# Five orders changed in a two-layer transformer kernel: queries and keys ahead of values in the first stage's middle chunks, and four reorderings further on

## The reference

```python
x = _layernorm(x + _L0_attn_ref(x, ...))  # 16 heads; half of each query and key gets rotary positions; causal softmax
x = _layernorm(x + _L0_ffn_ref(x, ...))   # shared expert plus the 2 best of 8 experts by sigmoid(x @ gate_w.T) + bias
x = _layernorm(x + _L1_attn_ref(x, ...))  # one head of width 512, biases, rotary positions on all of q and k
x = _layernorm(x + _L1_ffn_ref(x, ...))   # h = silu(x @ w_gate) * (x @ w_up); keep 2 of each 4 by size; h @ w_down
...
q_sem, k_sem = _split_heads(x @ Wq_sem.T, H), _split_heads(x @ Wk_sem.T, H)
q_geo, k_geo = _rope(_split_heads(x @ Wq_geo.T, H)), _rope(_split_heads(x @ Wk_geo.T, H))
v = _split_heads(x @ Wv.T, H)
```

## Time and profile before

| | |
|---|---|
| three runs | 2268.37, 2268.38 and 2271.72 us, median 2268.38 us |
| the profiled execution | span 2270.2 us; its own time 2271.96 us |
| PE busy in the span | 2172.7 us, 96% |
| DVE, ACT, POOL busy | 1191.6, 753.1, 670.4 us |
| mean granted clock of PE | 0.983 of full |
| layer0_qkv | 0 to 148.4 us |
| layer0_attention and layer0_project | 148.4 to 837 us |
| layer0_experts | 837 to 1149 us |
| layer1_attention | 1149 to 1713 us |
| layer1_mlp | 1713 to 2270 us |

### The profile page before, as it was taken

How to read it: one execution, slowest core, us unless ns; L and a number is a source line. 1 busy time by engine, 2 the same in 40 slices (tenths; PEclk the granted TensorE clock), 3 DMA queues, 4 the chain that set the end, 5 groups by cost and what they waited for, 6 DMA issues and landing times. The chain is left out here.

```text
span 2270.2 us, 27500 instructions
## 1 busy us (share of the span) xinstructions
PE 2172.7 (96%) x10148; PEld 1497.2 (66%) x10148; DVE 1191.6 (52%) x2324; ACT 753.1 (33%) x1351; POOL 670.4 (30%) x458
## 2 busy tenths in 40 slices
PE   8999999999999899999979999999998999999997
PEld 6876555555553644444457778888877888888885
DVE  6877677676661643222247542322236546554666
ACT  3325555555556332111134321111223221211223
POOL 5345555555556105332223250000003021211200
PEclk9989999999999999999999999999999999999999
DMA  5478245343300625555534460000101010100001
GB/s 198 176 204 199 81 118 132 95 89 71 71 15 21 247 79 211 136 115 90 85 105 142 149 231 20 28 19 19 47 1 56 1 38 19 38 18 18 19 19 56
DMA packets 104605, 197.27 MB, mean 87 GB/s; under 512 B 10385, under 2 KB 27665, under 8 KB 103057
## 3 DMA queue, kind: packets, MB, share of 16 engines
q1 hardware_dynamic: 92064, 162.78, 24.5%
q0 software_dynamic: 11408, 29.69, 5.8%
q10 hardware_dynamic: 1008, 3.15, 0.4%
HBM read 123.82 MB, written 71.75 MB: 86 GB/s over the span
## 5 line engine op out<-in xcount | busy, mean ns | idle before, releaser
L684 ACT ACTIVATE a_probs<-a_stb 128x512 f32<-128x512 f32 (+3 forms) x640 | 309.8, 535 | 240.6 <-PE a_stb L825 126.4
L650 POOL TENSOR_TENSOR a_probs<-a_probs 128x1024 f32<-128x1024 f32 (+3 forms) x158 | 278.4, 1775 | 247.5 <-PE a_avb L837 233.6
L722 DVE TENSOR_REDUCE a_mparts<-a_sbank 128x1 f32<-128x512 f32 x384 | 240.0, 683 | 86.3 <-PE a_sbank L799 86.1
L2207 POOL CAST m_wh<-wst 128x1024 fp32r<-128x1024 f32 x24 | 26.7, 1112 | 720.8 <-POOLq L1510 368.9
L57 PE MATMUL m_gu<-hi,m_wh 128*128 128x512 f32 x512 | 200.5, 392 | 4.7 <-DVE m_h L2282 2.8
L58 PE MATMUL m_gu<-lo,m_wh 128*128 128x512 f32 x512 | 199.9, 390 | 0.0
L59 PE MATMUL m_gu<-hi,m_wl 128*128 128x512 f32 x512 | 199.8, 390 | 0.0
L837 PE MATMUL a_avb<-a_probs,V 128*32 128x512 f32 (+3 forms) x1280 | 151.6, 546 | 0.7 <-ACT a_probs L684 0.7
L2282 DVE TENSOR_TENSOR m_h<-m_sg,m_gu 128x512 f32<-128x512 f32 x64 | 44.0, 688 | 193.8 <-ACT m_sg L2237 193.5
L727 DVE CUSTOM_DVE_ANT_0 a_junk<-a_sbank,hidden 128x128 bf16<-128x128 f32 (+3 forms) x256 | 113.4, 488 | 55.9 <-PE a_sbank L799 54.4
L799 PE MATMUL a_sbank<-hi,q 96*128 96x512 f32 (+3 forms) x304 | 119.4, 418 | 7.6 <-DVE a_mparts L722 4.2
(11 more groups left out here) (284 smaller groups left out, 4761.3 us busy)
## 6 DMA issues: line engine op xcount, KB each, us to landing
qk<-v_hl SPq DMA_DIRECT2D x32, 512.0 KB, 3.0
hi<-qk SPq DMA_DIRECT2D x60, 256.0 KB, 5.1
lo<-qk SPq DMA_DIRECT2D x60, 256.0 KB, 5.3
wst<-in_w_mlp SPq DMA_DIRECT2D x24, 512.0 KB, 3.5
q<-qk SPq DMA_DIRECT2D x42, 256.0 KB, 5.8
xs<-a_zeros POOLq DMA_DIRECT2D x39, 264.0 KB, 2.8
X<-xs SPq DMA_DIRECT2D x39, 264.0 KB, 2.7
v<-vhl SPq DMA_DIRECT2D x16, 512.0 KB, 5.1
```

Source lines behind the costliest of these rows:

```text
L650: nc.gpsimd.tensor_tensor(probs[:, i % PSLOTS, hs, w0:], probs[:, i % PSLOTS, hs, w0:], probs[:, (i + 1) % PSLOTS, hs, w0:], ALU.add)\
L684: nc.scalar.activation(probs[:, i % PSLOTS, h, w0:], stb[:, k % 3, w0:], ACT.Exp, scale=SCALE0)\
L722: nc.vector.reduce_max(to, sbank[:, b, :], AX).then_inc(s["unit_max"], 1)
```

## The change

Nothing is computed otherwise; five orders are changed.

1. layer0_qkv. In chunks 1 and 2 all four q/k groups are multiplied first (with the input event ahead of the last), then the four value tiles; so too in chunk 3, where the first value tile stood behind the second group. Chunk 0 keeps its order. ACT makes "high" one event later, DVE makes "low" behind the next group's shuffle. Piece 3 of the weights goes from POOL to ACT and DVE, and POOL splits pieces 2 and 4, then, behind the first cosines, 5.
2. layer0_project. "ranks" stands behind the event ("w", 3, 0) and not ahead of ("b", 1, 0).
3. The last two indirect additions, not one, are issued in layer1_attention.
4. layer1_attention. Other orders of ACT and DVE in its front and its chunks; bvr is loaded first.
5. layer1_mlp. In the first quarter DVE's product m_h of (c, r) = (1, 0) stands behind the first of the four low parts m_hl, not behind the fourth.

```diff
 layer0_qkv
+                if c > 0:
+                    return [("qk", c, 0), ("qk", c, 1), ("qk", c, 2), ("x", c + 1, 0), ("qk", c, 3)] + [("v", c, t) for t in range(TC)]
                 return ev + [("x", c + 1, 0), ("v", c, 1), ("qk", c, 3), ("v", c, 2), ("v", c, 3)]
-            return ev + [("qk", c, 3), ("v", c, 1), ("v", c, 2), ("v", c, 3)]
+            return [("qk", c, j) for j in range(NG)] + [("v", c, t) for t in range(TC)]
...
             split(2)
-            split(3)
+            split(4)
             for what, c, j in events:
                 if what == "qk":
                     cosines(c, j)
-                    if c == 0 and j < 2:
-                        split(4 + j)
+                    if c == 0 and j == 0:
+                        split(5)
...
-            last_qk = events.index(("qk", NC - 1, NG - 1))
-            acts = events[:last_qk + 3] + [("high", NC - 1, NG - 1)] + events[last_qk + 3:]
+            acts = []
+            for i, ev in enumerate(events):
+                acts.append(ev)
+                if i > 0 and events[i - 1][0] == "qk":
+                    acts.append(("high", *events[i - 1][1:]))
...
+                            if i == 4:
+                                split(3)
...
+            for i, (what, c, j) in enumerate(events):
+                swapped = [ev for ev in events[:i] if ev[0] == "qk"][-1:] if what != "v" else []
+                held = [("low", *ev[1:]) for ev in swapped if ("low", *ev[1:]) not in steps]
+                if what == "qk":
+                    steps += [("swap", c, j)] + held + [("sum", c, j)]
+                elif what == "x":
+                    steps += [("x", c, j)] + held
+            steps.append(("low", NC - 1, NG - 1))
 layer0_project
-            ev += [("ranks", 0, -1)] * before + [("b", 1, 0), ("w", 3, 0)]
+            ev += [("b", 1, 0), ("w", 3, 0)] + [("ranks", 0, -1)] * before
 layer0_experts and layer1_attention (LATE = 2)
-            for j in range(NR - 1):
+            for j in range(NR - LATE):
...
-            pool.wait_ge(added, 16 * (NR - 1))
-            nc.gpsimd.indirect_dma_start(acc_dram[:, :], bass.IndirectOffsetOnAxis(ap=last_to, axis=0), last_rows, None,
-                                         compute_op=ALU.add).then_inc(added, 16)
+            for i in range(LATE):
+                pool.wait_ge(added, 16 * (NR - LATE + i))
+                nc.gpsimd.indirect_dma_start(acc_dram[:, :], bass.IndirectOffsetOnAxis(ap=last_to[i], axis=0), last_rows[i],
+                                             None, compute_op=ALU.add).then_inc(added, 16)
 layer1_attention, DVE in a chunk (ACT likewise)
-                if c + 1 < NC:
-                    stats(n)
-                    stats(n + 1)
-                    apply(n)
-                    apply(n + 1)
-                sines(p)
...
+                for t, tiles in enumerate(((n,), (n + 1, n + 2), (n + 3,))):
+                    sines(p + t)
+                    for k in tiles if c + 1 < NC else ():
+                        stats(k)
+                    sums(p + t)
+                    for k in tiles if c + 1 < NC else ():
+                        apply(k)
+                    low(p + t)
 layer1_mlp
+                            if c == 0 and r == 0 and is_first(q):
+                                dve.wait_ge(s["hl_ok"], 1)
+                                dve.wait_ge(s["sg_ok"], 5)
+                                tt(h[:, 0, :], sg[:], gu[:, 0, 1, :], ALU.mult).then_inc(s["h_ok"], 1)
```

More of the change, by code:

```diff
@@ L293, in split @@
             def split(i):
-                act.wait_ge(wload[i], 16)
-                nc.scalar.activation(piece_of(i, wqh, wvh), wst[:, i, :], ACT.Copy).then_inc(s["whi_a"], 1)
+                act.wait_ge(wload[i % 3], 16 * (i // 3 + 1))
+                nc.scalar.activation(piece_of(i, wqh, wvh), wst[:, i % 3, :], ACT.Copy).then_inc(s["whi_a"], 1)
             def split_half(a):
@@ L330, in _ @@
                     nc.scalar.activation(qkf[:, k % 2], qk[:, k % 2], ACT.Copy).then_inc(s["qkf_ok"], 1)
-                if what == "high" or (what == "qk" and k < NC * NG - 1):
+                elif what == "high":
                     act.wait_ge(s["sum_ok"], k + 1)
@@ L358, in _ @@
             split_half(0)
-            for what, c, j in events:
+            steps = []
+            for i, (what, c, j) in enumerate(events):
[6 more added lines that the diff above has]
+            steps.append(("low", NC - 1, NG - 1))
+            for what, c, j in steps:
                 k = c * NG + j
@@ L368, in _ @@
                         split(1)
-                elif what == "qk":
+                        split(3)
+                elif what == "swap":
                     dve.wait_ge(s["qkf_ok"], k + 1)
@@ L373, in _ @@
                     nc.vector.stream_shuffle(rotated[:], qkf[:, k % 2], SWAP).then_inc(s["rot_ok"], 1)
+                elif what == "sum":
                     if j == 0:
@@ L381, in _ @@
                     tt(t1[:, k % 2], t1[:, k % 2], rotated[:], ALU.add).then_inc(s["sum_ok"], 1)
+                elif what == "low":
                     dve.wait_ge(s["hi_ok"], k + 1)
@@ L914 @@
 AHEAD = 2
+LATE = 2
 def shared_up(nc, w0, xt, ab, c, j):
@@ L1033, in run @@
                         act.wait_ge(s["gt_ok"], g + 1)
+                        if not opening:
+                            act.wait_ge(s["sm_ok"], g)
                         nc.scalar.activation(sig[:].rearrange("p t e -> p (t e)"), sb8[:, 0:TC * NE],
@@ L1496, in _ @@
             down(NR - 1, old)
-    return s["added"], y[:, (NR - 1) % 2, :], to[:, NR - 1:NR]
+    late = range(NR - LATE, NR)
+    return s["added"], [y[:, j % 2, :] for j in late], [to[:, j:j + 1] for j in late]
 READY = 12
@@ L1721, in _ @@
                 weight(0, d)
+            fuse(0)
             act.wait_ge(s["bias_in"], 16)
             nc.scalar.activation(bvh, bvr[:].unsqueeze(2).broadcast_to([P, ND, P]), ACT.Copy).then_inc(s["bvh_ok"], 1)
-            fuse(0)
-            weight(1, 0)
-            weight(1, 1)
             fuse(1)
-            weight(1, 2)
-            weight(1, 3)
+            fuse(2)
+            for d in range(ND):
+                weight(1, d)
+            fuse(3)
+            nc.scalar.activation(nrm.std[:, NT - 1:NT], nrm.eps[:], ACT.Sqrt)
+            fuse(ND)
             root(0)
-            fuse(2)
             apply(0)
             root(1)
+            apply(1)
             turn(0)
-            apply(1)
-            fuse(3)
             root(2)
+            apply(2)
             turn(1)
-            apply(2)
-            fuse(ND)
             root(3)
@@ L2028, in scores @@
                     last.then_inc(s["s_ok"], 1)
-            for j in range(3):
+            for j in range(ND + 1):
                 fuse(j)
             turn(0)
-            fuse(3)
             turn(1)
-            fuse(ND)
             value(0)
@@ L2278, in run @@
                     elif what == "up":
+                        if (c, r) == (1, 0) and is_first(q):
+                            continue
                         if r == 0 and not (c == 0 and is_first(q)):
+                            dve.wait_ge(s["hl_ok"], i * 4)
+                        if r == 1 and c == 1 and is_first(q):
                             dve.wait_ge(s["hl_ok"], i * 4)
```

55 lines of the change are left out of this document (21 added, 34 removed).

## The result

The changed kernel takes 2278.35 us in the median of 6 runs (2277.6 to 2286.03), the kernel before 2270.05 in the median of 6 (2267.84 to 2276.9); the ratio is 1.004, 95% interval 1.0024 to 1.0056. It is slower by about 9 us, as forecast (2275.2, range 2263 to 2283). The profiled execution was the slowest of the six, 2286.03 us with a span of 2284.2, so it shows 14.0 us more than the span of before.

| stage | before | after | difference |
|---|---|---|---|
| layer0_qkv | 148.5 | 168.0 | +19.5 |
| layer0_attention | 591.7 | 592.8 | +1.1 |
| layer0_project | 97.3 | 97.5 | +0.2 |
| layer0_experts | 311.7 | 307.2 | -4.5 |
| layer1_attention | 564.0 | 562.9 | -1.1 |

A forecast was written before the change was run, and what follows sets the result against it. The prediction took PE, busy nearly throughout, to bound the kernel, so only its waits count. Terms of +14.5 - 0.8 - 3.3 - 0.9 - 2.7 = +6.8 on the median 2268.4 gave 2275.2 us, range 2263 to 2283.

The forecast's parts named there:

- Middle chunks: layer0_qkv, chunks 1 and 2: value tile 3 waits 5.25 us for ACT's copy, plus a clock drop, each; +13.5 us.
- Start: layer0_qkv, chunk 0: the wait at 26.2 goes, tile 3 waits 5.0 as DVE is late; chunk 1 starts 1.5 us later.
- End: layer0_qkv, last chunk: tile 3 waits 1.5, the wait at the barrier shrinks from 3.1 to 1.0; together -0.5 us.
- 1.5 each: layer0_qkv, middle chunks: a clock drop behind each long PE wait costs 1.5 us beside the wait.
- layer0_project: PE's wait moves from p_xn to otl, -0.4 us in each of two chunks; -0.8 us.
- Border and front: Border of the experts: barrier about 4.9 us earlier, additions in series, the wait for q_wl and its drop gone; -3.3 us.
- Projection chunks: Second layer's projection: q_across wait goes, waits of 1.7 for xl and 1.4 for values come per chunk; -0.9 us.
- MLP: layer1_mlp: the wait of 2.8 for m_h becomes 1.6 and its clock drop goes; -2.7 us.
- Rival A: layer0_qkv: DVE keeps up, tile 3 waits 0.5 without a drop; total -9.7, 2258.7 us; chance 0.15.
- B: Waits as forecast but half the size, few clock drops; stage 1 +5 to +8, total about 0; chance 0.27.
- D: Edits behind stage 1 do nothing: layer0_project's wait changes name, serial additions hold the front; 2281 us; chance 0.1.
- C: Projection chunks: the new order brings short waits that lower the clock each time; +4.5 over forecast, 2279.7 us; chance 0.13.

The follow-up runs named there:

- the version with the copies first: Changed kernel, but in chunks 1 to 3 ACT copies value tiles 1 and 2 ahead of the last group's high part: 2265.13 us, ratio 0.999.
- short cosines: Changed kernel, but POOL's product with the cosines covers 64 of 512 columns per half from the third group on: 2266.27 us, ratio 0.9985.
- the order alone: Kernel before, with only all four q/k groups ahead of the four value tiles in chunks 1 and 2: 2294.53 us, ratio 1.0105.
- the version with the old pieces: Changed kernel with the middle chunks' old order and the weight pieces split as before; high and low keep new places: 2262.39 us, ratio 0.9957.
- the versions with the old ranks: Changed kernel, ranks in old place: with ACT's value copies ahead of high parts in all chunks, ratio 1.0003; with layer0_qkv as before, 0.9981.

## Why the prediction was right

**Middle chunks, +13.5.** Right in mechanism, place and size: waits of 5.18 and 5.19 for 5.25 forecast. The whole of it in time, from the versions with and without the new order, is 14 us (10 to 18). All three links were shown apart: ACT's list (the version with the copies first takes the wait away), POOL's hold on DVE (short cosines: 5.2 to 1.5), and DVE's pace (the order alone: 9.0).

**Start, +1.5.** The wait at 26.2 went, one of 4.66 came in chunk 0 (5.0 forecast). The cause named, piece 4's landing with POOL idle before it, is borne out by the version with the old pieces, with the first sum 3.3 us earlier. The size was off: chunk 1 starts at 50.09 us where it started at 47.11, 3.0 later and not 1.5, mainly since the drop behind the wait was the longer kind. The piece was there at 19.1 us, not at 18.5.

**End, -0.5.** 1.43 for the last tile and 1.20 at the barrier, forecast 1.5 and 1.0.

**The term that was mis-sized** is the clock: "1.5 each" behind a wait. The five waits of this stage sum to 17.7 us, 18.0 by the forecast; before there were 2.78 and 3.13. That is +11.8 of the stage's +19.5. Three drops at 2.65 make 8.0, against one of 1.5: +6.5 where the forecast had +3.0. The last 1.2 us lie at the same places: over 24 steps, from 85.69 to 94.02, the drop costs 2.87, and the step into each wait is 0.16 longer than the idle time shown (77.62 to 85.69 are 12 steps and 5.18 of idle, 8.07 in all, where 12 steps take 2.73). By parts the stage is +3.0 for the start, +16.4 for the two middle chunks and +0.2 for the end. By the ratios it costs 17.5 us in a mean run, 3 over the forecast of 14.5, which the intervals (12.5 to 22.5) can't tell apart. The trace of before had a drop of the longer kind too, in layer0_project, behind the wait of 2.80 for p_xn; the forecast had read only the one behind 26.2:

```profile
777.20:783.40 6.20, 6.10 (x16) 4.48 (x16) 3.94 (x7) 1.34 (x4) 0.59 (x1) 0.50 1.01 401
```

**layer0_project, -0.8.** The step "the wait moves from one name to the other" held, but otl now takes 3.06 of PE's time, not 2.4: the sum is +0.2, and nothing was gained in this trace. In time the new place may be worth more than the 0.8, by the clock (see the versions with the old ranks), which the forecast did not have. The second name in my text was right, its size was not: the sigmoid let DVE begin the ranks only 0.7 us after p_xn was done.

**Border and front, -3.3.** The barrier came 4.5 us earlier (4.9 forecast), the loads of acc when forecast.

**Projection chunks, -0.9.** The wait for q_across is gone, and 1.56 for q_xcl and 1.18 for values came (1.7 and 1.4). layer1_attention changed by -1.1 in the profiled execution, where front and chunks behind the barrier were forecast at +0.7. No time shows the gain of the new orders.

**MLP, -2.7.** The wait is 1.57 (1.6) and no drop follows it. But a drop now followed the waits of 2.22 and 1.90 at the stage's start, which had none before: -1.3 in this trace. In the version with stage 1 as before, which had no drop there, the MLP took 554.2 us, 2.9 less than before.

That the four later edits came to -8 against -7.7 is right in sum; that their parts do so is shown by no time, and there is some luck in it.

Rival A (DVE keeps up) fell with the two waits; B with their size; D held for layer0_project alone, and there only in the trace; C, short waits that lower the clock, happened in part: in the changed kernel twice in three chunks.

## What to carry to other kernels

Before work is put ahead in PE's list, ask which instruction on the copying engine's list now stands ahead of the copy that frees PE's buffer, and when its input is ready; a copy that is ready need not wait behind a part that is not. Where DVE and POOL share a stage, price DVE's two-operand instructions with POOL's time over them, and by where they stand: moving one moves the loss, it does not remove it. The versions to keep are those with the middle chunks' old order: with the old weight pieces 0.9957, or with the whole stage as before 0.9963; they can't be told apart. When a wait only changes its name, its price can still change by the clock behind it: compare times too, and more than one trace.

## What the runs showed of the hardware

One drop of PE's clock had two sizes: seven steps in 3.06 us, a loss of 1.5, and 16 steps in 6.29 us, a loss of 2.65, with nothing in the program between them that would tell which. Nor is the wait's length a sure sign: in the changed kernel the clock fell behind waits of 1.56 and 1.18 us at 1225 and 1228, but not behind the same pair at 1265, and behind 2.22 and 1.90 us at 1728 and 1732, which had no drop in the kernel before. Over the twelve traces a drop followed all 22 waits of 3.8 us or more (the program's first wait, for its inputs, apart). Of the 42 waits of 2.9 to 3.3 us outside the first opening of the attention, 27 had one. The order alone waited 3.26 us at 26.25, more than the 2.78 of the earlier trace rows, and stayed at full clock, 13 matmuls in the window where before had 7:

```profile
26.20:29.20 3.00, 2.95 (x13) 2.41 (x14) 2.97 (x4) 0.00 (x0) 3.00 (x1) 1.00 0.74 279
```

Of the nine waits of 4.6 us or more, eight were followed by 6.75 us or more at half clock, so for waits like those forecast here the longer drop is the one to price. Executions of the kernel before spread over 2264 to 2278 us, and the stretches at half clock are the part of such a spread that the traces show: the attention, which no version changes, took 589.1 to 597.7 us, with its opening at the lower clock for 24 to 38 us.

That DVE and POOL hold each other up was expected; the trace put numbers on it. In one list, with one shape, the low part took 1.25 us without long POOL work and 2.42 with it, up to 3.44 when both began within 0.24 us of each other. The Trainium skill ("SBUF — State Buffer", section "SBUF: two separate sides") calls that an exclusive lock in which the later one blocks. By that rule POOL's own stretch, 2.60 and up to 3.34 for 2.42 alone, should also come from a DVE instruction with two SBUF inputs already under way. The trace agrees: POOL's cosines of 3.05 us began at 108.93, while DVE's sum ran from 108.47 to 109.70. It was not tried apart.
